# Tensor arithmetic of an adaLN block moved from GpSimd to VectorE, setup loads reordered, instruction orders written anew

## The reference

```python
mod = (silu(c) @ wmod).reshape(16, 6, 1, -1)          # sa, ca, ga, sb, cb, gb
ga = (2*(ga >= 0) - 1) * max(abs(ga), 0.25)           # gb likewise
h = layernorm(x) * (1 + ca) + sa
# attention: scores |q k^T| / 16 under a causal mask, softmax, out = weights @ v, then Wo
x = x + ga * attention(h, Wq, bq, Wk, bk, Wv, bv, Wo, bo)
h = layernorm(x) * (1 + cb) + sb
# ffn: every row picks one of 64 "tiles" by scores against cluster and tile signatures,
#      a 2-16-1 spline gives a magnitude mag, and y = h + mag * directions[tile] * scale
#      ffn(h) = layernorm(y) * gamma + beta
x = x + gb * ffn(h)
```

## Time and profile before

| | us |
|---|---|
| median of 3 runs | 457.81 (455.69 to 460.1) |
| the profiled execution, its own time | 455.52 |
| its span in the trace | 453.7 |
| PE busy | 398.9 (88%) |
| DVE busy | 380.3 (84%) |
| ACT busy | 299.8 (66%) |
| POOL busy | 58.4 (13%) |

### The profile page before, as it was taken

How to read it: one execution, slowest core, us unless ns; L and a number is a source line. 1 busy time by engine, 2 the same in 40 slices (tenths; PEclk the granted TensorE clock), 3 DMA queues, 4 the chain that set the end, 5 groups by cost and what they waited for, 6 DMA issues and landing times.

```text
span 453.7 us, 7812 instructions
## 1 busy us (share of the span) xinstructions
PE 398.9 (88%) x2129; PEld 309.6 (68%) x2129; DVE 380.3 (84%) x1384; ACT 299.8 (66%) x656; POOL 58.4 (13%) x97
## 2 busy tenths in 40 slices
PE   8999999999999996999999999999999999835030
PEld 8876776877877784776877787778867777724020
DVE  3785666279698989899889989998999899998996
ACT  2246739796898594858894789569965886746020
POOL 4028311010000013020110013000220110011132
PEclk9999999999999996999999999999999999957555
DMA  8720341042103304353452305530451260015342
GB/s 241 215 53 27 121 163 46 1 116 92 25 1 116 95 32 62 61 127 116 72 93 94 116 17 113 128 94 1 71 116 47 33 109 1 1 35 82 61 63 84
DMA packets 32906, 35.65 MB, mean 79 GB/s; under 512 B 3370, under 2 KB 28448, under 8 KB 32864
## 3 DMA queue, kind: packets, MB, share of 16 engines
q1 hardware_dynamic: 24752, 26.88, 19.7%
q0 software_dynamic: 7536, 7.48, 12.2%
q10 hardware_dynamic: 576, 0.80, 0.5%
HBM read 19.36 MB, written 15.79 MB: 77 GB/s over the span
## 4 chain that ended last, share of the span: by engine, by line
PE 76%; DVE 12%; ACT 6%; issue 5%; DVEq 0%; ACTq 0%; POOL 0%; POOLq 0%
PE bank L603 14%; PE bank L620 13%; PE bank L580 12%; PE bank L593 11%; PE bank L642 6%; PE bank L611 3%; PE bank L629 3%; PE bank L568 3%; PE bank L682 2%; DVE y L2319 2%; PE bank L443 2%; DVE res L2333 1%; PE bank L673 1%; ACT L1207 1%; DVE sp L2277 1%
## 5 line engine op out<-in xcount | busy, mean ns | idle before, releaser
L620 PE MATMUL bank<-v,probsT 128*128 128x257 f32 x320 | 79.5, 382 | 1.5 <-ACT probsT L1284 1.0
L603 PE MATMUL bank<-h,g 128*128 128x128 f32 (+3 forms) x256 | 78.2, 436 | 1.3 <-ACT gath L1356 0.8
L593 PE MATMUL bank<-m_ga,h 128*128 128x258 f32 x256 | 66.2, 384 | 0.8 <-DVE negmax L2148 0.8
L620 PEld LDWEIGHTS bank<-v,probsT 128*128 128x128 f32 x320 | 57.6, 190 | 12.1 <-issue 2.6
L580 PE MATMUL bank<-h,a_sb 128*128 128x512 f32 x128 | 62.1, 609 | 3.7 <-DVE cmp_t L2268 3.7
L593 PEld LDWEIGHTS bank<-m_ga,h 128*128 128x128 f32 x256 | 46.3, 192 | 13.2 <-issue 6.3
L603 PEld LDWEIGHTS bank<-h,g 128*128 128x128 f32 x256 | 42.8, 190 | 17.7 <-issue 9.3
L2035 POOL DMA_DIRECT2D out<-res x14 | 18.1, 1295 | 279.8 <-DVE res L2333 279.8
L2148 DVE CUSTOM_DVE_ANT_0 probs<-bank,cmask 128x128 f32<-128x128 f32 (+1 forms) x64 | 31.0, 484 | 18.1 <-ACT bank L1273 17.8
L1266 ACT ACTIVATE g<-bank,g_bias 128x512 f32<-128x512 f32 x32 | 21.9, 688 | 33.0 <-PE bank L580 32.9
L1273 ACT ACTIVATE bank<-bank,v 128x128 f32<-128x128 f32 (+1 forms) x64 | 31.6, 500 | 11.9 <-PE bank L603 10.5
(11 more groups left out here) (183 smaller groups left out, 808.6 us busy)
## 6 DMA issues: line engine op xcount, KB each, us to landing
x<-in_L_attn_x SPq DMA_DIRECT2D x16, 512.0 KB, 4.0
out<-x SPq DMA_DIRECT2D x14, 512.0 KB, 4.9
out<-res POOLq DMA_DIRECT2D x14, 512.0 KB, 6.4
gb_row<-gate_rows SPq DMA_DIRECT2D x16, 256.0 KB, 3.5
a_row<-gate_rows SPq DMA_DIRECT2D x14, 256.0 KB, 3.3
out<-res SPq DMA_DIRECT2D x2, 512.0 KB, 3.6
wide<-in_L_wmod SPq DMA_DIRECT2D x1, 768.0 KB, 11.9
wide<-in_L_wmod ACTq DMA_DIRECT2D x1, 512.0 KB, 5.8
```

Of the source, the lines that this page charges most:

```text
L593: last = mm(ps[:, 0:VW], h[s][:, c, t * P:(t + 1) * P], m_ga[p % 2][s][:, c, :], start=(c == 0), stop=(c == KC - 1))
L603: last = mm(ps[:, 0:w], g[s][:, c, t * P:(t + 1) * P], h[s][:, c, 0:w], start=(c == 0), stop=(c == KC - 1))
L620: last = mm(ps[:, 0:D + 1], probsT[s][t][:, j * P:(j + 1) * P], v_sb[s][:, j, 0:D + 1], start=(j == 0), stop=(j == t))
```

## The change

`ms` and `base` become functions of the DVE block, with the same waits and the same operands, and their calls are placed in DVE's list. GpSimd keeps `sp_sig` and `sp_rest` of the setup and the 14 DMAs `ay`. The load of `in_mod_ga` goes from the ACT queue to the SP queue, behind Wq and Wk and behind a wait of SP for `in_mod`. The matmuls of `busy` go from 8 and 16 to 4 and 9. `BANK` is assigned anew (`G11`, `HD` and `CM` still share one), and the lists of SP, PE, ACT and DVE have other orders.

```diff
             load(x_ld[0][0], x_sb[0][0][:, :, :], x_v[0])
             weight(in_qk, wq, "Wq")
             weight(in_qk, wk, "Wk")
+
+            spq.wait_ge(in_mod, 16)
+            load(in_mod_ga, wmod_sb[:, :, 2 * D:3 * D], wmod_v[:, :, 2 * D:3 * D])
             weight(in_o, wo, "Wo")
             weight(in_v, wv, "Wv")
...
             load(in_mod, wmod_sb[:, :, 0:2 * D], wmod_v[:, :, 0:2 * D])
             exp_table()
-            load(in_mod_ga, wmod_sb[:, :, 2 * D:3 * D], wmod_v[:, :, 2 * D:3 * D])
...
-                busy(BUSY_BANK, 8)
+                busy(BUSY_BANK, 4)
...
-                busy(BUSY_BANK, 16)
+                busy(BUSY_BANK, 9)
...
-            def ms(p, s):
...
-                    pool.wait_ge(ga_ld[p % 2][s], 16 * ((p + 1) // 2))
-                need(pool, v_done, NT * seq(p - 2, s) + NT)
-                tt(m_ga[p % 2][s][:, :, 0:D], m_sb[:, :, :],
-                   a_row[p % 2][s][:, 0:D].unsqueeze(1).broadcast_to([P, KC, D]), ALU.mult).then_inc(ms_rdy, 1)
...
+            def ms(p, s):
...
+                    dve.wait_ge(ga_ld[p % 2][s], 16 * ((p + 1) // 2))
+                need(dve, v_done, NT * seq(p - 2, s) + NT)
+                tt(m_ga[p % 2][s][:, :, 0:D], m_sb[:, :, :],
+                   a_row[p % 2][s][:, 0:D].unsqueeze(1).broadcast_to([P, KC, D]), ALU.mult).then_inc(ms_rdy, 1)
+
+            def base(g, u):
...
+                dve.wait_ge(summed[0], 16 * BY_SUM)
+                need(dve, sent, 16 * (g - BY_SUM))
+                tt(res[:, 2 * u:2 * u + 2, :], x2[p % 2][s][:, t, :],
+                   gb_row[g % 2][u // 2][:, 1:2, :].broadcast_to([P, 2, D]), ALU.add).then_inc(base_rdy, 1)
```

More of the change, by code:

```diff
@@ L2681, in _ @@
             loc(1, 5)
+            y_(0, 1)
+            loc(1, 6)
             b_ri(2, 1, 0)
+            y_st(0, 0)
+            loc(1, 7)
+            b_ttr(2, 1, 3)
+            b_ri(2, 1, 1)
+            b_x2(2, 1, 0)
+            a_st(4, 0, 0)
+            y_st(0, 1)
+            a_st(4, 0, 1)
+            b_st(2, 1, 0)
+            y_(0, 2)
+            b_ri(2, 1, 2)
+            loc(1, 8)
+            for i in range(1, 3):
+                b_x2(2, 1, i)
+            a_st(4, 0, 2)
             y_(0, 3)
-            y_st(0, 1)
@@ new lines, in _ @@
+            y_st(2, 1)
+            loc(3, 2)
+            for i in range(1, 3):
+                a_st(6, 0, i)
+            b_ri(4, 1, 1)
+            a_st(6, 0, 3)
+            for i in range(2, 4):
+                y_(2, i)
+            b_x2(4, 1, 1)
+            b_ri(4, 1, 2)
+            b_st(4, 1, 0)
+            b_x2(4, 1, 2)
+            b_st(4, 1, 1)
+            b_ri(4, 1, 3)
+            b_st(4, 1, 2)
+            y_(2, 4)
+            b_x2(4, 1, 3)
+            y_st(2, 2)
+            b_st(4, 1, 3)
@@ new lines, in _ @@
+            clc(4, 7)
+            c_b2(3)
+            clc(4, 8)
+            ob(2, 5)
+            clc(4, 9)
+            b_ttr(5, 1, 1)
+            clb(4, 0)
+            b_x2(5, 0, 1)
+            clb(4, 1)
+            b_ri(5, 0, 2)
+            b_v(5, 1, 3)
+            spl(3, 0)
+            b_x2(5, 0, 2)
+            spl(3, 1)
+            b_st(5, 0, 1)
+            clb(4, 2)
+            b_ttr(5, 1, 2)
+            spl(3, 2)
+            clb(4, 3)
+            spl(3, 3)
+            clb(4, 4)
@@ L3134, in _ @@
+            y_(3, 1)
+            b_ri(5, 1, 2)
+            y_st(3, 0)
+            a_st(7, 0, 0)
+            b_ri(5, 1, 3)
+            b_st(5, 1, 1)
+            loc(4, 0)
+            b_x2(5, 1, 2)
+            for i in range(1, 3):
+                a_st(7, 0, i)
+            b_x2(5, 1, 3)
+            y_(3, 2)
+            b_st(5, 1, 2)
+            loc(4, 1)
+            b_st(5, 1, 3)
+            y_(3, 3)
+            loc(4, 2)
+            c_var(5, 0)
+            ob(2, 7)
             for i in range(1, 4):
@@ L3135, in _ @@
                 c_var(5, i)
[L3136 to L3137 removed]
+            y_(3, 4)
+            loc(4, 3)
+            y_(3, 5)
+            y_st(3, 1)
             c_nw(5, 0)
[L3139 removed]
+            loc(4, 4)
             c_nw(5, 1)
@@ new lines, in _ @@
+            loc(5, 0)
+            b_x2(6, 1, 2)
+            b_ri(6, 1, 3)
+            loc(5, 1)
+            b_st(6, 1, 1)
+            b_x2(6, 1, 3)
+            for i in range(2, 4):
+                b_st(6, 1, i)
+            y_st(4, 0)
+            c_var(6, 0)
+            y_st(4, 1)
+            y_(4, 4)
+            loc(5, 2)
+            y_(4, 5)
+            for i in range(1, 4):
+                c_var(6, i)
+            b_v(7, 0, 0)
+            y_st(4, 2)
+            loc(5, 3)
+            ob(3, 6)
@@ new lines, in _ @@
+            y_st(7, 1)
+            lob(8, 2)
+            for i in range(4, 6):
+                ob(6, i)
+            lob(8, 3)
+            y_(7, 3)
+            y_st(7, 2)
+            oa(6, 7)
+            lob(8, 4)
+            y_st(7, 3)
+            oh(8, 0)
+            y_var(7, 0)
+            oh(8, 1)
+            y_var(7, 1)
+            ob(6, 6)
+            for i in range(2, 4):
+                y_var(7, i)
+            oa(7, 0)
+            for i in range(0, 2):
+                base(7, i)
```

2866 lines of the change are left out of this document (1365 added, 1501 removed), and 16 rows, old and new, of the table BANK.

## The result

The changed kernel takes 455.14 us (median of 18 runs, 453.96 to 456.12) where the kernel before took 457.96 beside it (18 runs, 455.69 to 460.28): ratio 0.9937, 95% interval 0.992 to 0.9955. It is 2.8 us faster, less than the 1% that I had set as the bound of "faster". The profiled execution has an own time of 455.40 us against 455.52 before, so the two traces show a difference of 0.1 us, not of 2.8.

What follows compares the result with a forecast made beforehand. PE was taken to bound the kernel until pair 6's last `b_x2` (341.4 us), then DVE. Terms -5.6 - 1.4 + 0 + 0.7 + 0.9 = -5.4 gave 450.1 us profiled, 452.4 median; range 445 to 460.5.

Steps and rivals of the forecast that it cites:

- Stalls in PE's part: PE idle at 170 us goes, -5.6 us; three DVE stalls from 279 to 334 us go, -1.4.
- `ms` on DVE: 16 `ms` cost DVE 9.6 us ahead of pair 6's last `b_x2`, hidden in its free time: 0.
- The hole: PE idle 3.7 us until 174.20, then four matmuls at lower clock, 1.9 more: 5.6 us, expected to go.
- New waits on DVE: `ms` waiting for gate rows in DVE's in-order list: loads fit in time, 0, bounds 0 and 1.5 us.
- DVE's end: Behind pair 6's last `b_x2`: 4.9 us of added calls against 4.2 held, +0.7, bounds -1.8 and +3.5.
- Setup: First `S_` behind `sd_rest`, last small load at 24.8 us as now: +0.9 us, bounds -2.0 and +7.5.
- setup late: Rival: SP's wait shifts later loads 4.7 us, first `S_` at 32.6, half clock: +7.5, 459.0 us; chance 0.05.
- The rest: New bank assignment and orders priced at 0 as long as PE's part stays full.
- The bank rival: PE meets `CM`'s bank unread by DVE in groups 0 to 4, two 5.6 us holes: 463.6 us; chance 0.09.
- DVE decided all along: Rival: DVE's work from 150 us on sets the end, 15.7 us held come back: 447.3 us; chance 0.22.
- Nothing at the hole: Rival: another wait holds PE where the stall did, DVE's end keeps +0.7: 458.5 us; chance 0.08.

Runs made afterwards that it cites:

- the move alone: Kernel before with `ms` and `base` moved to VectorE, other engines' orders, banks and loads as before: 449.42 us, ratio 0.9821.
- `sd_rest` later: Changed kernel with one call moved: `sd_rest` behind `b_ttr(0, 0, 2)` instead of ahead of `sd_nw(1)` and `ms(0, 0)`: 449.65 us, ratio 0.9824.
- the kernel with 12 us less on VectorE: Changed kernel with `ms` and `base` put back on GpSimd, in a reordered list: 459.12 us, ratio 1.0033.
- the kernel with the gap: Kernel before with one wait added: each `ms` on GpSimd waits for the `ms` before it: 453.99 us, ratio 0.992.
- `ms` spread: Kernel before with only GpSimd's list reordered, `ms` calls taken out from behind the waiting `ay` stores: 450.33 us, ratio 0.9845.
- the lone multiplications: Kernel before with `ms` and `base` on VectorE, plus 15 unused multiplications on GpSimd, each alone: 449.39 us, ratio 0.9824.
- `sd_rest` early in the orders of before: Kernel before with `ms` and `base` on VectorE and `sd_rest` right behind `sd_bias`: 451.26 us, ratio 0.9864.

## Why the prediction was right or wrong

The direction and the range (445 to 460.5) held, but the range is 15.5 us wide, and I had given "within 1%", where it came out, 0.36 only. The size didn't hold: 5.4 us forecast for the profiled execution, 0.1 measured, and 2.8 between the medians. Step by step:

*Stalls in PE's part (-5.6 - 1.4) and `ms` on DVE (0)* were right. With the move alone, the time from pair 0 to pair 6 (table) falls from 277.89 to 270.57 us, by 7.3 against 7.0 forecast, and its pair 6 stands at 335.31, where I had put the changed kernel's (to the digit by luck, since its pair 0 is 1.2 us late and not 0.9). The hole is worth 6.0 there (pair 2 to pair 3: 52.22 to 46.21), pairs 4 to 6 take 1.3 less. Only my reason was half: it takes the issue of an `ay` with `ms` directly behind it to hold one instruction for 4 us, and the `ms` stood there ready because `ay(0, 0)` waited ahead of them.

*New waits on DVE (0)*: right, no `ms` waited.

*DVE's end (+0.7)*: right within its bounds. From pair 6 to the last `ob` it takes 108.4 us before, 108.0 changed, 108.8 with the move alone.

*Setup (+0.9)* is the first step that failed: it measured +3.8 by pair 0 between the two traces, and +1.6 to +3.5 against the six other kernels with the loads, the empty matmuls and the `sd_rest` of before, which reach pair 0 at 63.85 to 65.74 us. I had seen `sd_rest` move ahead and priced it, but from a landing at 24.8 us, "as now", on the reading that SP had issued ahead of what the memory delivered. It landed at 26.0, and with the load back on ACT at 23.3. The rival "setup late" had the mechanism, wait and half clock, with the landing at 29.5; the truth lay between. I also underrated what the new orders and the fewer empty matmuls bring here without that wait: 26.57 us for the first `b_v` against 29.09 before and 30.03 with the move alone, beyond my bound of -2.0. So the place of one call costs 5.5 us against the same kernel without it.

*The rest (0)* failed too: "priced at 0 as long as PE's part stays full". It doesn't stay full. From pair 0 to pair 6 the changed kernel gains 3.6 us, not 7.0. With `sd_rest` later it gains 5.3; TensorE has new waits of 0.9, 1.2 and 1.1 us near 171, 222 and 270 us there, which the move alone hasn't; which of the new orders or banks makes them stays open. The last 1.7 us is a half clock in the profiled execution (below). The bank rival, two holes of 5.6 us, didn't happen.

*"DVE decided all along"* is out: the kernel with 12 us less on VectorE was slower. *"Nothing at the hole"* is out by the table.

*The median.* "I carry the difference over unchanged" (2.3 us between the profiled execution and the median) was wrong: the profiled execution of before, 455.52 us, is quicker than every one of the 18 runs (455.69 and up). The traces show one place where that can come from. From the last `b_x2` of pair 7 to `ob(6, 3)` it takes 31.0 us in the profiled execution of before, and 31.0 and 31.2 in two kernels with its lists; in six others with those lists it takes 32.9 to 33.7. The difference is TensorE's clock in that stretch. Windows of the kernel with the gap, quick, then of the one with `ms` spread, slow, both 9 to 17 us behind that `b_x2`:

```profile
401.72:405.72 4.00, 2.79 (x12) 2.42 (x12) 4.00 (x14) 0.94 (x3) 1.28 (x1) 0.50 0.17 53
405.72:409.72 4.00, 2.68 (x24) 2.54 (x24) 4.00 (x16) 2.15 (x7) 0.00 (x0) 1.00 0.95 146
```

```profile
398.17:402.17 4.00, 2.79 (x12) 2.42 (x12) 4.00 (x14) 0.94 (x3) 1.28 (x1) 0.50 0.18 54
402.17:406.17 4.00, 2.66 (x12) 2.69 (x13) 4.00 (x16) 1.66 (x4) 0.00 (x0) 0.50 0.95 145
```

In 4 us the one does 24 matmuls and the other 12. The profiled execution of before was a lucky one by 2.4 us against the median of 18, and that is how 0.1 between two traces goes with 2.8 between two medians, and 5.7 for the move alone with 8.3. That this stretch was its luck is argued, not shown: the two other quick kernels (the gap, and the lone multiplications) have their profiled executions at the median of their runs, and all five kernels with the new orders take 30.9 us there, so being quick there may belong to a kernel's timing and not to chance. Pair 0 at 63.50 us, earlier than in all six other kernels with that setup, is another part of it.

The fastest kernels of the study are at 449.0 to 449.7 us, 1.8% under the kernel before and 1.2% under the changed one: the move alone, and the change with `sd_rest` later.

## What to carry to other kernels

A call that waits for a late load, put ahead in an in-order list, costs what every engine behind that list loses, here 5.5 us for three instructions of 0.15 us; ask of each moved wait what its landing is, to the microsecond, and don't reuse today's landing when the queue ahead of it changes. When GpSimd's list puts ready arithmetic behind a waiting DMA issue, it comes out in a bunch directly behind the issue; try a reordering (worth 7.4 us here), or one wait between (3.9), before moving the work. And compare a trace with the spread of its runs before trusting a difference of 1 or 2 us between two single executions.

## What the runs showed of the hardware that was not expected

TensorE's clock can fall after a wait of about 1 us, and not every time. The same sequence at the same 1.06 us hole, in the changed kernel and in the one with `sd_rest` later:

```profile
276.04 0.74 PE L676 MATMUL bank<-table,onehotT 128*128 128x322 f32 x2 [1.06 <-ACT gath L1356]
276.62 1.79 PE L623 MATMUL bank<-v,probsT 128*128 128x257 f32 x6
278.21 1.06 PE L653 MATMUL bank<-ident,pre 128*128 128x128 f32 x4
279.06 2.44 PE L606 MATMUL bank<-h,g 128*128 128x384 f32 x4
```

```profile
270.57 0.74 PE L676 MATMUL bank<-table,onehotT 128*128 128x322 f32 x2 [1.06 <-ACT gath L1356]
271.16 1.46 PE L623 MATMUL bank<-v,probsT 128*128 128x257 f32 x6
272.46 0.60 PE L653 MATMUL bank<-ident,pre 128*128 128x128 f32 x4
272.89 1.46 PE L606 MATMUL bank<-h,g 128*128 128x384 f32 x4
```

It cost 1.7 us in three of the five profiled executions with this order and nothing in two; in those two the clock fell at 378 and 382 us instead, some 2 us after a wait of 1.08 us. It fell as well after the 1.10 us with the load on the ACT queue and the 1.22 us with the gap, and it stayed after 1.18 us with `sd_rest` early in the orders of before. Ahead of the hole above stand eight matmuls of 4 columns; what decides I can't say.

A VectorE instruction that meets GpSimd issuing a DMA with arithmetic directly behind it is held over both, and over all of a bunch there: 4.36 us for one beside an `ay` and three `ms`, 2.74 beside an `ay` and one. A gap of 0.17 us between two `ms` is enough to let it go. Without an issue ahead, operations that follow without a gap held one instruction each (1.51 and 1.23 us beside two `base`).
